# A graph attention layer on one core: copied rows and turned sums later in the order, a last step in two parts, a bias before its wait

## What is computed

```python
h = jnp.maximum(_layernorm(x), 0.0)
q = (h @ Wq.T + bq).reshape(N, 8, 16); v = (h @ Wv.T + bv).reshape(N, 8, 16)
k = (edge_h @ Wk.T + bk).reshape(-1, 8, 16)
in_m, out_m, diag_m = sum(q[src] * k), sum(q[dst] * k), sum(q[src] * q[dst])      # over 16
score = (segment_softmax(in_m / 4, dst) + segment_softmax(out_m / 4, dst)
         + segment_softmax(diag_m / 4, dst)) * distance ** lam
out = segment_sum(score[..., None] * v[dst], dst).reshape(N, 128) @ Wo.T + bo
return x + leaky_relu(out, 0.1)
```

## Time and profile before

| | us |
|---|---|
| median of 3 runs | 3112.04 (3103.01 to 3129.29) |
| the profiled execution | 3131.95 |
| its span, first to last instruction | 3130.1 |
| scans of the first and the last unit (L1017) | at 258.0 and 2902.7 |

### The profile page before, as it was taken

One profiled execution on the slowest core, in us unless ns is written; L12 is line 12 of the kernel. 1 busy time (PEld: TensorE's weight loads), 2 busy tenths in 40 slices (PEclk: granted clock), 3 DMA queues, 4 the chain that ended last, 5 costly groups with the idle time before them and its releaser, 6 DMA issues.

```text
span 3130.1 us, 42543 instructions
## 1 busy us (share of the span) xinstructions
PE 1948.4 (62%) x10766; PEld 1130.7 (36%) x10766; DVE 1746.2 (56%) x2897; ACT 900.6 (29%) x1929; POOL 1778.5 (57%) x1869
## 2 busy tenths in 40 slices
PE   2526666666666666666676666666666566665247
PEld 1423333333333333333333333333333343333125
DVE  2536655556556555555665555655565565655435
ACT  1412233333233323323332232322232233333011
POOL 6165555566555655555665655665555655653552
PEclk7767888888788887878888888887788888888556
DMA  4467555656555655655665665655555555652234
GB/s 136 161 163 227 154 174 173 190 172 187 172 174 176 179 172 176 175 171 176 183 183 174 190 178 179 181 176 173 173 173 175 176 176 175 178 181 90 92 91 140
DMA packets 395524, 527.87 MB, mean 169 GB/s; under 512 B 82285, under 2 KB 301297, under 8 KB 382178
## 3 DMA queue, kind: packets, MB, share of 16 engines
q1 hardware_dynamic: 312546, 336.44, 33.7%
q0 software_dynamic: 59616, 119.35, 16.5%
q10 hardware_dynamic: 23328, 71.72, 6.1%
HBM read 442.67 MB, written 84.57 MB: 168 GB/s over the span
## 4 chain that ended last, share of the span: by engine, by line
PE 36%; another core or an unknown queue 25%; issue 22%; DVE 9%; ACT 6%; ACTq 1%; SPq 1%; DMA 1%; DVEq 0%
PE qd_ps L824 10%; PE k_ps L813 9%; PE lg_ps L803 6%; PE t_ps L844 4%; PE qs_ps L833 3%; DVE prod L1006 3%; ACT rows L921 2%; DVE onehot L992 2%; ACT kq L891 2%; DVE max_ps L1017 2%; DVE prod L1002 1%; PE z_ps L1281 1%; PE z_ps L1279 1%; PE qv_ps L395 1%
## 5 line engine op out<-in xcount | busy, mean ns | idle before, releaser
L148 POOL DMA_INDIRECT qsrc<-q_tab,idx_sb x1664 | 1589.5, 955 | 1088.2 <-issue 474.6
L824 PE MATMUL qd_ps<-onehot,window 128*128 128x128 f32 x3328 | 570.1, 327 | 367.5 <-ACT kq L897 176.0
L1002 DVE SCALAR_TENSOR_TENSOR prod<-k_ps,bk_col,kq 128x512 f32<-128x512 f32 x416 | 311.0, 748 | 779.5 <-remote 326.2
L824 PEld LDWEIGHTS qd_ps<-onehot,window 128*128 128x128 f32 x3328 | 515.5, 236 | 397.4 <-issue 366.6
L897 ACT COPY kq<-qd_ps 128x512 f32<-128x512 f32 x416 | 243.8, 586 | 1380.5 <-remote 808.3
L813 PE MATMUL k_ps<-ea_sb,wk_sb 128*128 128x512 f32 x832 | 535.3, 732 | 35.2 <-DMA ea_sb<-in_ea 35.2
L1006 DVE TENSOR_TENSOR prod<-qs_ps,kq 128x1024 f32<-128x1024 f32 x416 | 505.8, 1216 | 65.3 <-remote 53.1
L844 PE MATMUL t_ps<-ident,sums 128*128 128x128 f32 x936 | 189.9, 319 | 516.5 <-ACT rows L921 297.9
L803 PE MATMUL lg_ps<-prod,heads 128*32 128x384 f32 x3328 | 397.4, 541 | 16.3 <-issue 16.1
L891 ACT ACTIVATE kq<-k_ps,bk_col 128x512 f32<-128x512 f32 x416 | 286.8, 689 | 265.4 <-PE k_ps L813 128.6
L844 PEld LDWEIGHTS t_ps<-ident,sums 128*128 128x128 f32 x936 | 117.6, 158 | 557.2 <-ACT rows L921 287.4
(11 more groups left out here) (147 smaller groups left out, 1047.1 us busy)
## 6 DMA issues: line engine op xcount, KB each, us to landing
ea_sb<-in_ea SPq DMA_DIRECT2D x104, 1024.0 KB
window<-q_tab SPq DMA_DIRECT2D x1664, 64.0 KB
state<-rows ACTq DMA_DIRECT2D x104, 576.0 KB
near_sb<-near_tab SPq DMA_DIRECT2D x104, 512.0 KB
pa_sb<-pa_tab SPq DMA_DIRECT2D x104, 258.0 KB
qsrc<-q_tab,idx_sb POOLq DMA_INDIRECT x1664
xs<-in_x SPq DMA_DIRECT2D x28, 448.0 KB
q_tab<-qs SPq DMA_DIRECT2D x14, 448.0 KB, 2.5
```

The source lines that it names most:

```text
L148: pool.indirect_dma_start(out=qsrc[:, r, j, :], out_offset=None, in_=q_tab, in_offset=bass.IndirectOffsetOnAxis(ap=idx_sb[:, q, g * GRP + ...
L824: t = nc.tensor.matmul(qd_ps[:, at], window[:, r, j, :], onehot[:, m % 2, at], start=True, stop=True)
L1002: nc.vector.scalar_tensor_tensor(out=prod[:, g % 2, 2, :], in0=k_ps[:, g % 2, :], scalar=bk_col[:, 0:1], in1=kq[:, g % 2, 1, :], op0=ALU.a ...
```

## The change

Three edits. In the edge pass, PE does `turn_sums` after the picks, keys and head sums of its group instead of ahead of them, and in g = 1 the head sums come last. ACT copies the first turned rows ahead of `take_max`. In the out pass the last step is cut into one of five columns and one of two (`WIDE`), and PE makes the bias before it waits for the copied rows.

```diff
+WIDE = (HALF,) * (NSTEP - 1) + (5, HALF - 5)
+FROM = tuple(sum(WIDE[:k]) for k in range(len(WIDE)))
...
             def unit(h, q):
                 v = scanned(h, q)
                 for g in range(NG):
-                    if g < 3 and v is not None and (not isinstance(v, int) or v > 0):
-                        turn_sums(v - 1, q % 2, g)
                     if exists(h, q, g + 1):
                         pick(h, q, g + 1)
                         keys(h, q, g + 1)
...
-                    if exists(h, q, g - 1):
+                    if exists(h, q, g - 1) and g != 1:
                         sums_of_heads(h, q, g - 1)
+                    if g < 3 and v is not None and (not isinstance(v, int) or v > 0):
+                        turn_sums(v - 1, q % 2, g)
                     if exists(h, q, g + 1):
                         turn(h, q, g + 1)
+                    if g == 1:
+                        sums_of_heads(h, q, g - 1)
...
                     if g == 0 and v is not None:
                         seed(v)
-                        take_max(v, 1 - q % 2)
                     if g < 2 and done:
                         take_rows(v - 1, q % 2, g)
+                    if g == 0 and v is not None:
+                        take_max(v, 1 - q % 2)
...
             def project(k, b):
+                need(pe, res_ready, k - 1)
+                wide = tiles(k)[1]
+                for j in range(0, wide, GRP):
+                    n = min(GRP, wide - j)
+                    nc.tensor.matmul(z_ps[:, b, j:j + n, :], ones[:, :], bo_sb[:, 0:n, :], start=True, stop=False)
                 pe.wait_ge(hvT_copied, k + 1)
-                need(pe, res_ready, k - 1)
-                for j in range(0, HALF, GRP):
-                    n = min(GRP, HALF - j)
-                    nc.tensor.matmul(z_ps[:, b, j:j + n, :], ones[:, :], bo_sb[:, 0:n, :], start=True, stop=False)
-                for j in range(HALF):
+                for j in range(wide):
                     m = nc.tensor.matmul(z_ps[:, b, j, :], hvT[:, b, j, :], wo_sb[:, :], start=False,
-                                         stop=j in (GRP - 1, HALF - 1))
+                                         stop=j in (GRP - 1, wide - 1))
                 m.then_inc(z_ready, 1)
```

More of the change, by code:

```diff
@@ L153, in fetch_results @@
         def fetch_results(pool, k):
-            for j in range(HALF):
-                at = k * HALF + j + 1
+            for j in range(WIDE[k]):
+                at = FROM[k] + j + 1
                 pool.indirect_dma_start(out=st[:, k % RST, j, :], out_offset=None, in_=state,
@@ L1245, in out_pass, with tiles, columns @@
         block = env["block"]
+        NS = len(WIDE)
+        def tiles(k):
+            return (k * HALF, HALF) if not isinstance(k, int) else (FROM[k], WIDE[k])
+        def columns(k):
+            at, n = tiles(k)
+            return bass.ds(at * F, n * F)
         @block.sync
@@ L1252, in _ @@
                 sp.dma_start(bo_sb[:, j, :], env["bo"]).then_inc(wo_in, 16)
-            for k in range(NSTEP):
-                r = k % RST
+            for k in range(NS):
+                r, n = k % RST, WIDE[k]
                 need(sp, res_ready, k - RST + 1)
-                sp.dma_start(vs[:, r, :, :], v_v[:, k * HALF * F:(k + 1) * HALF * F]).then_inc(in_sem[r], 16)
-                sp.dma_start(xs[:, r, :, :], x_v[:, k * HALF * F:(k + 1) * HALF * F]).then_inc(in_sem[r], 16)
+                sp.dma_start(vs[:, r, 0:n, :], v_v[:, columns(k)]).then_inc(in_sem[r], 16)
+                sp.dma_start(xs[:, r, 0:n, :], x_v[:, columns(k)]).then_inc(in_sem[r], 16)
         @block.gpsimd
         def _(pool):
-            for k in range(RST, NSTEP):
+            for k in range(RST, NS):
                 pool.wait_ge(step[1], k - RST + 1)
@@ L1269, in turn @@
                 pe.wait_ge(hv_ready, k + 1)
-                for j in range(HALF):
+                for j in range(tiles(k)[1]):
                     t = nc.tensor.transpose(hT_ps[:, b, j, :], hv[:, b, j, :], ident[:, :])
@@ L1291, in _ @@
             project(1, 1)
-            with pe.Fori(1, NSTEP // 2) as w:
+            with pe.Fori(1, NS // 2 - 1) as w:
                 for b in range(2):
@@ L1295, in _ @@
                     project(2 * w + b, b)
+            for k in range(2 * (NS // 2 - 1), NS):
+                turn(k, k % 2)
+                project(k, k % 2)
         @block.scalar
@@ L1300, in copy @@
                 act.wait_ge(hvT_ready, k + 1)
-                nc.scalar.copy(hvT[:, b, :, :], hT_ps[:, b, 0:HALF, :]).then_inc(hvT_copied, 1)
+                n = tiles(k)[1]
+                nc.scalar.copy(hvT[:, b, 0:n, :], hT_ps[:, b, 0:n, :]).then_inc(hvT_copied, 1)
             def store(k, b):
                 act.wait_ge(res_ready, k + 1)
-                act.dma_start(out_v[:, bass.ds(k * HALF * F, HALF * F)], res[:, b, :, :]).then_inc(res_out[b], 16)
+                act.dma_start(out_v[:, columns(k)], res[:, b, 0:tiles(k)[1], :]).then_inc(res_out[b], 16)
             def take_z(k, b):
@@ L1315, in _ @@
             take_z(0, 0)
-            with act.Fori(1, NSTEP // 2) as w:
+            with act.Fori(1, NS // 2 - 1) as w:
                 copy(2 * w, 0)
@@ L1322, in _ @@
                 store(2 * w - 1, 1)
[L1323 to L1327, removed]
+            for k in range(2 * (NS // 2 - 1), NS):
+                copy(k, k % 2)
+                take_z(k - 1, (k - 1) % 2)
+                store(k - 2, k % 2)
+            take_z(NS - 1, (NS - 1) % 2)
+            store(NS - 2, NS % 2)
+            store(NS - 1, (NS - 1) % 2)
+            act.wait_ge(res_out[0], 16 * (NS - NS // 2))
+            act.wait_ge(res_out[1], 16 * (NS // 2))
         @block.vector
@@ L1368, in _ @@
                     finish(k - 2, (k - 2) // 2, k % 2)
-            for k in range(NSTEP - 2, NSTEP):
+            finish(NS - 3, (NS - 3) // 2, (NS - 3) % 2)
+            scores(NS - 1, (NS - 1) // 2, (NS - 1) % 2)
+            for k in range(NS - 2, NS):
                 finish(k, k // 2, k % 2)
```

35 lines of the change are left out of this document (19 added, 16 removed).

## The result

| | before | after |
|---|---|---|
| median, same chip | 3116.11 us (3103.01 to 3129.29, 4 runs) | 3017.34 us (3014.35 to 3018.40, 4 runs) |
| ratio | | 0.9681, 95% interval 0.9638 to 0.9725 |
| span of the profiled execution | 3130.1 | 3016.6 |
| first scan, last scan | 258.0, 2902.7 | 253.6, 2803.7 |
| edge pass, scan to scan | 2644.7 | 2550.1 |

The kernel became 3.2% faster (3004 was forecast). 2644.7 - 2550.1 = 94.6 us of it lie in the edge pass, 0.92 us in each of 103 intervals, and 14.5 us behind the last scan. Before the first scan lie 4.4 us, in a pass that the change doesn't touch.

What follows compares the result with a forecast made beforehand. No engine is full; a chain of waits bounds the kernel, with PE's signals held while POOL gathers. Gains of 92 (edge pass), 14 (bias) and 2 (split last step) make 108: 3112 - 108 = 3004 us, range 2870 to 3120.

Steps and rivals of the forecast that it cites:

- The bound: Edge pass: a unit is POOL's gathers, 20.1 us, plus its pauses, 5.7; PE's signals are held while POOL gathers.
- rival 2: Edge pass unchanged, POOL's pattern stays or PE really works until 1573.2; only the out pass gains, 3096 us; chance 0.23.
- The moved instructions: Edge pass: PE starts 1.8 us sooner, the pick 2.5; 0.9 us a unit gained, 92 us in all (bounds 0 and 255).
- The irregular units: Edge pass: units off the steady 24.8 us, with a mean of 25.7 over all units, were to disappear, gaining 0.9 a unit.
- the steady unit: Edge pass: two runs of eight gathers, each with one pause, 12.4 us each, make 24.8 us; this was to remain.
- rival 1: Edge pass: signals flow better, one of two pauses falls away in most units; 23.2 us a unit, 2841 us; chance 0.20.
- ACT's waits behind the later turned sums: Edge pass: ACT's `take_rows` k = 2 waits behind head sums; costs nothing if signals are prompt, otherwise up to 1.8 us.
- The exchange in g = 1: Edge pass: head sums go behind turn and `turn_sums`, about 0.9 + 0.7 us later relative to the pick.
- rival 3: Edge pass slower: longer runs of gathers hold signals longer, 0.6 us a unit, 61 us more; 3157 us; chance 0.12.
- The out pass: Bias ahead of the copied rows gains 14 us (bounds 0 and 26); last step in two gains 2 (-3 to +4).
- The sum: Whole kernel: 92 + 14 + 2 = 108 us gained, from 3112 to 3004 us.

Runs made afterwards that it cites:

- the ring of 16: The changed kernel with a ring of 16 groups for the gathered rows instead of 8; 3660.02 us, 1.1667 of the kernel before.
- out_pass_only: The kernel before with only the out pass edits (bias ahead of the copied rows, last step in two); 3132.71 us, ratio 0.9995.

## Why the prediction was right, and where not

- **The bound.** Signals held by gathers, POOL's runs and pauses: shown, by the fillers in place of gathers and by the chip on which signals come through; the ring of 16 agrees. The prediction had the signals held whenever POOL gathers. That is too broad: the first four gathers of a run let most of them pass, in the very stretch that it read (1564.71). How the gathers hold them stays open. What I missed besides is that this is no property of the kernel alone. In four of the five sets of runs the kernel before took 3116 to 3139 us, in one 2393. The forecast's mechanism holds on the first kind; on the other, rival 2 (no change in the edge pass) is the truth, for another reason than I gave it: POOL's floor of 20.1 us is the bound.
- **The moved instructions, 0.9 us a unit, 92 us.** Measured 0.92 and 94.6 by the first profiles; against the old order in out_pass_only (2632.5) it is 0.80 and 82.4. The pick's start behind the one-hot, the turned sums' idle and POOL's (986.8, forecast about 1000) came as said. Two steps under it did not. The irregular units have not disappeared: the scans below lie 27.7, 23.6, 24.5 and 24.1 apart, and the mean of 24.8 is a mixture that happens to meet the steady unit. Counted in POOL's timeline from 400 to 2700 (a pause is over 1 us without a gather), there were 232 pauses of 2.42 us on average, and now 196 of 2.46: they are fewer and no shorter. Before, 119 of POOL's runs between pauses had eight gathers and 85 had four; now 157 have eight and 23 four. That is where the gain lies, and it is partly rival 1's mechanism (a pause falls away in some units) in a smaller size. So the size of 0.9 was met in part by luck. And the prediction read the stall as one of ACT's order (`take_rows` behind `take_max`); the runs give that 17 to 29 us alone and PE's move 75 to 88.

  DVE in the timeline of the changed kernel, 1500 to 1600, as the earlier trace rows:

```profile
1499.96 0.97 DVE L1022 TENSOR_TENSOR_SCAN max_ps<-pa_sb,lg_ps 128x387 f32<-128x387 f32 x1 [0.21 <-ACT terms L908]
1527.66 0.97 DVE L1022 TENSOR_TENSOR_SCAN max_ps<-pa_sb,lg_ps 128x387 f32<-128x387 f32 x1 [1.42 <-PE t_ps L846]
1551.23 0.97 DVE L1022 TENSOR_TENSOR_SCAN max_ps<-pa_sb,lg_ps 128x387 f32<-128x387 f32 x1 [1.21 <-issue]
1575.73 0.97 DVE L1022 TENSOR_TENSOR_SCAN max_ps<-pa_sb,lg_ps 128x387 f32<-128x387 f32 x1 [0.90 <-ACT terms L908]
1599.82 0.97 DVE L1022 TENSOR_TENSOR_SCAN max_ps<-pa_sb,lg_ps 128x387 f32<-128x387 f32 x1 [0.58 <-issue]
```

- **ACT's waits behind the later turned sums** cost nothing that shows. The exchange in g = 1, which the prediction weighed in rival 3, is worth nothing that can be told on either kind of chip.
- **The out pass, 14 and 2 us.** From the last scan to the end 227.4 became 212.9, 14.5 us; over three profiles of the old out pass (227.4, 225.4, 224.3) and three of the new (212.8, 213.8, 212.9) it is 225.7 - 213.2 = 12.5. The times do not show it whole: out_pass_only allows 12 us at most, and on the second kind the out pass was worth 4.6. Parted they were only there: 2.9 and 1.7, the second not clear of noise. How the 12.5 divide on the first kind stays open; the rows of the out pass after (the bias made inside waits of 38.48 and 19.65 us) speak for the bias, as the prediction had it.
- **The sum.** 108 us forecast, 113.5 between the two spans, 98.8 between the medians. The profiled execution of before (3131.95) was longer than all four in the table, so the stage's 94.6 us are on the high side. The range, 2870 to 3120, was wider than it needed to be on this chip, and its lower end, 2870, lies 480 us above what the changed kernel took on the other.
- **Rivals.** Rival 1 (POOL's idle at 850 or below) did not come. Rival 3's mechanism, longer runs that hold signals longer, has its likeness in the ring of 16, but the change brought few runs of over eight gathers (11, where there were 7).

## What to carry to other kernels

Ask of each wait whether its signal comes from PE while GpSimd issues gathers back to back. Where such signals are late, put PE's work that is ready ahead of any PE instruction that waits for another engine's answer. Don't let GpSimd run further ahead without measuring it (a longer ring made this kernel 17% slower). Shorter runs, or work between the gathers, weren't tried with all gathers kept. Judge such a change on more than one chip: the same program took 2393 and 3116 us, and an edit worth 3% on one kind was worth 0.1% on the other. A wait of an engine that isn't the bound may be long at little cost (240 us before the turned sums cost about 2).

## What the runs showed of the hardware that was not expected

- In four of the five sets of runs PE signals came late while GpSimd issued indirect DMAs back to back: 15.1 us (1667.18 to 1682.27) in a run of 16, where the signal came 0.08 us after the last one; in the unit shown of the changed kernel it came 1.90 us after. Signals of the first four gathers of a run mostly passed in under 0.1 us (150 of 175), later ones hardly ever (3 of 140). Three fills of 0.91 us each (2.74 us) in place of gathers held nothing. In the hold of the longer ring the DMA engines were 22% busy.
- Late in such runs or just behind them, PE's own instructions also stood still for 0.3 to 1.8 us with no wait that the profile shows (29 times in the turns of the kernel before, never on the second kind of chip).
- In the fifth the same program showed no such wait, its gathers took the same time (951 ns), and it ran 23% faster. What parts the two kinds, the chip itself or something in the way executions are set up or recorded on it, isn't told by these runs.
- The kernel before spread over 36 us in 12 of 13 runs on one chip of the first kind (47 with the longest), the changed one over 4 us in its 4, and both over 6 to 8 us on the other kind. Which units fall irregular seems to differ from execution to execution; that was argued, not shown.
